# Moving the key-value products of one batch to another place among the next batch's matmuls

## The chip, the cores and the metric

The kernel runs on one core of a Trainium2 chip. The metric is the device time of one launch in microseconds, the median of several runs. TensorE (PE in the profile) does the matmuls, ScalarE (ACT), VectorE (DVE) and GpSimd (POOL) the rest, and SyncE (SP) issues the DMAs. Every engine works through its own fixed list of instructions and waits on semaphores for the others.

## What is computed

Eight batches of 256 rows by 512 columns go through linear cross attention with 16 heads, and then through a feed-forward layer with quantised activations and ternary weights. Cut to what matters here:

```
q, k, v = heads(layernorm(x) @ Wq.T + bq), heads(ctx @ Wk.T + bk), heads(ctx @ Wv.T + bv)
q_prime = relu(q @ Wqf.T)                 # 64 features per head
k_prime = relu(k @ Wkf.T) * mask
kv      = einsum('bhnf,bhne->bhfe', k_prime, v)       # "products of features and values"
k_sum   = k_prime.sum(rows)
x       = x + (q_prime @ kv / (q_prime @ k_sum + 1e-8)) @ Wo.T + bo
# feed-forward: weights and activations quantised, wq(w) has values -1, 0, 1 times mean|w|
h       = bit_linear(layernorm(x), w_up) * relu(bit_linear(layernorm(x), w_gate))**2
x       = x + bit_linear(rms(h) * subln_weight, w_down)
```

## The kernel before

The whole program is unrolled. Python first writes a list of steps (class `Plan`, lines 93 to 237); each has a lane (pe, act, dve, pool, sp), a cost, and the steps it waits for. The PE lane is executed in the order in which the steps were added. The order on the other lanes is worked out by `Plan.queues` (line 108): it simulates the engines with the costs of the table `COST` (line 55) and gives each engine, whenever it is free, the step that can start first, and among these the one that is needed first. The order is fixed when the kernel is built, so moving a step on the PE lane may also reorder the other lanes.

The work falls in two stages. First, for each batch b from 0 to 6, the loop at lines 840 to 855 adds to the PE lane:

- `keys(b)` (line 504): 48 matmuls of 128x256, each product in three parts (high*high, high*low, low*high). ACT then adds the bias and copies the result from PSUM to SBUF (`kT{b}.*.all`). Below K0, K1, ...
- `values(b, t)` for t = 0 and 1 (line 527): two halves of 12 matmuls of 128x512 each. DVE adds the bias and writes the rows (`v{b}.{t}.rows`). Below V0, V1, ... for the two halves together.
- `kv(b - 1)` (line 573): the products of the features and values of the batch before; 64 steps in fp32, of which each becomes two matmuls, 128 small ones of 33 columns. They wait for the four `kf{b-1}.{r}.rows` of DVE and for the rows of the values, write PSUM banks 0 and 1, and ACT copies them out (`kv{b-1}.0`, `kv{b-1}.1`). Below kv0, kv1, ...
- `features(b)` (line 549): 64 steps, again 128 small matmuls, of 64 columns, into banks 0 to 3; they wait for the keys' copies and for whoever used those banks last. DVE turns them into `kf{b}.{r}.rows` (line 567). Below F0, F1, ...

So in the kernel before, the PE order of a batch is keys, first half of the values, products of the batch before, second half of the values, features. `means(b, stage)` (line 481) stands between them. After three of these places it sets a weight of the feed-forward layer (gate, up, down) to ternary: DVE adds up four partial sums (`w{w}.sum`), a one-column matmul on PE (`w{w}.all`, line 470) adds them over partitions, DVE makes mean and scale, ACT multiplies four chunks of the weight (`w{w}.{c}.fma`), DVE rounds them (`w{w}.{c}.min`, `.tern`). The place (5, "kv") belongs to the down weight; each `.min` that finishes frees a 1 MB slot into which SP loads `x` or `Wo` for the next stage.

The last batch (7) and the second stage are written out by hand in `FLOW` (line 41), word by word: K is `keys`, V a range of the 24 value matmuls, F `features`, P `kv`, X transposes of normalised rows, L layer norm statistics, W queries, Q query features, A the attention products, S the output projection, G, U and D the feed-forward matmuls; `@` lists the PSUM banks to use.

Each PE matmul is two instructions, a weight load (LDWEIGHTS) and the matmul itself. At the start 13 matmuls warm PE up.

Of the kernel before, what the change touches and what calls it, by code (L numbers as in the profile page):

```python
# [38 lines left out]


FLOW = (
# [198 lines left out]
def xattn_bitffn_kernel(nc, x_d, ctx_d, wk_d, wv_d, wq_d, wo_d, feat_d, small_d, bv_d, bo_d, g_d, wg_d, wu_d, wd_d, out_d):  # L240
# [4 lines left out]
    with ExitStack() as es:  # L245
# [16 lines left out]
        AM, SXI, SX, SX3, CC, C2, S0, S1, SS, VE, RS, CRS, M0, M1, MX, SYI, SO, KK = range(18)  # L262
# [84 lines left out]
        def dma(name, mb, waits, out, in_, sem):  # L347
            if sem not in dma_names:
                dma_names.append(sem)
            return add("sp", name, 2.9 * mb, waits, lambda e: e.dma_start(out, in_), sem)  # L350

        def mm(name, cost, waits, out, lhsT, rhs, start, stop):
            return add("pe", name, cost, waits, lambda e: e.matmul(out, lhsT, rhs, start=start, stop=stop))  # L353
# [4 lines left out]
        def tt(lane, name, cost, waits, out, a, b, op):  # L358
            return add(lane, name, cost, waits, lambda e: e.tensor_tensor(out, a, b, op))  # L359

        def ts(lane, name, cost, waits, out, a, s1, s2, op0, op1):
            return add(lane, name, cost, waits, lambda e: e.tensor_scalar(out, a, s1, s2, op0, op1))  # L362
# [26 lines left out]
        def load_slot(name, s, src):  # L389
            return dma(name, 1.0, slot_user[s], slot[s], src, f"slot{s}")  # L390
# [22 lines left out]
        def ctx_load(b, n=1):  # L413
            w = KC * T // n
            for h in range(n):
                c = slice(w * h, w * h + w)
                dma(f"ctx{b}.in{h}", 0.5 / n, ctx_lo[b - 2] if b > 1 else [], craw[:, b % 2, c], ctx_d[b][:, c], f"ctx{b % 2}.{h}")

        def ctx_split(b, n=1):
            war = [f"v{b - 2}.1.3.2"] if b > 1 else []  # L420
            w = KC * T // n
            ctx_lo[b] = []
            for h in range(n):
                o = slice(w * h, w * h + w)
                c = slice(1024 * (b % 2) + w * h, 1024 * (b % 2) + w * h + w)
                act(f"ctx{b}.hi{h}", 0.06 + w * 8.7e-4, [f"ctx{b}.in{h}"] + war, aph[:, c], craw[:, b % 2, o], ACT.Copy)
                ctx_lo[b].append(tt("dve", f"ctx{b}.lo{h}", 0.07 + w * 1.04e-3, [f"ctx{b}.in{h}", f"ctx{b}.hi{h}"] + war, apl[:, c], craw[:, b % 2, o], f32(aph[:, c]), ALU.subtract))
# [30 lines left out]
        def ternary_load(w):  # L458
            for c in range(4):
                s = chunk_slot[c]  # L460
                ld = load_slot(f"w{w}.{c}", s, raw_d[w][:, c * 2048:c * 2048 + 2048])
                act(f"w{w}.{c}.abs", 1.85, [ld], tern[w][:, c * 2048:c * 2048 + 2048], slot[s], ACT.Abs, accum_out=wsum[:, 4 * w + c:4 * w + c + 1])

        def ternary(w, b):
            q = 4 * w
            add("dve", f"w{w}.sum", 0.07, [f"w{w}.{c}.abs" for c in range(4)],
                lambda e: e.tensor_reduce(wst[:, q:q + 1], wsum[:, q:q + 4], AX_X, ALU.add))

            total = ps[:, b, 511:512]
            mm(f"w{w}.all", 0.25, [f"w{w}.sum", "ones"] + bank_user[b], total, wst[:, q:q + 1].broadcast_to((P, P)), vt[:, 0, 0, 32:33], True, True)  # L470
            bank_user[b] = [ts("dve", f"w{w}.mean", 0.1, [f"w{w}.all"], wst[:, q + 2:q + 3], total, 1.0 / (FI * H), 1e-5, ALU.mult, ALU.max)]
            recip(f"w{w}.scale", 0.07, [f"w{w}.mean"], wst[:, q + 3:q + 4], wst[:, q + 2:q + 3])
            for c in range(4):
                s = chunk_slot[c]
                t = tern[w][:, c * 2048:c * 2048 + 2048]
                act(f"w{w}.{c}.fma", 1.95, [f"w{w}.scale", f"w{w}.{c}.abs", "cm0"], slot[s], slot[s], ACT.Identity, scale=wst[:, q + 3:q + 4], bias=cm[:, 0:1])
                ts("dve", f"w{w}.{c}.min", 1.13, [f"w{w}.{c}.fma"], t, slot[s], MAGIC, 1.0, ALU.subtract, ALU.min)
                slot_user[s] = [f"w{w}.{c}.min"]
                add("dve", f"w{w}.{c}.tern", 0.6, [f"w{w}.{c}.min"], lambda e, t=t: e.tensor_scalar(t, t, -1.0, None, ALU.max))

        def means(b, stage):

            if (b, stage) in TERNARY_AFTER:
                w = TERNARY_AFTER.index((b, stage))
                ternary(w, {"keys": 4, "kv": 2, "values": 6}[stage])
                if w < 2:
                    ternary_load(w + 1)
                else:
                    ts("pool", "CW", 0.3, ["w0.mean", "w1.mean"], CW, Mg, Mg, Mu, ALU.mult, ALU.mult)
                    load_slot("Wo", 3, wo_d)  # L490
                    for n in range(6):
                        dma(f"x{n}", 0.5, slot_user[n // 2], xs[:, 2 * n:2 * n + 2, :], x_d[n], f"x{n}")
                    ln1(0)
# [33 lines left out]
        def values(b, t):  # L527

            c0 = 1024 * (b % 2)
            out = ps[:, 4 + t, :]  # L530
            calls = []
            for kc in range(KC):
                cs = slice(c0 + T * kc + P * t, c0 + T * kc + P * t + P)
                for z in range(3):
                    def call(kc=kc, cs=cs, z=z):
                        waits = [Wv_lo[kc]] + ctx_lo[b] + (bank_user[4 + t] if kc == z == 0 else [])
                        left, right = apl if z == 2 else aph, wol if z == 1 else woh
                        last = kc == KC - 1 and z == 2
                        (open_banks.remove if last else open_banks.add)(4 + t)
                        k = mm(f"v{b}.{t}.{kc}.{z}", 0.23, waits, out, left[:, cs], right[:, kc, :], kc == z == 0, last)  # L540
                        if last:
                            dst = vt[:, (2 * b + t) % 4, :, :].rearrange("p a (c d) -> p a c d", c=2)[:, :, :, 0:32]
                            src = out.rearrange("p (a c d) -> p a c d", a=NP, c=2)
                            bvv = bv_b[:, :].rearrange("p (a c d) -> p a c d", a=NP, c=2)
                            bank_user[4 + t] = [tt("dve", f"v{b}.{t}.rows", 0.62, [k, "bv", "ones"], dst, src, bvv, ALU.add)]
                    calls.append(call)
            return calls
# [63 lines left out]
        def ln1(a):  # L611
            for t in range(2):
                i = 2 * a + t
                r = ln_stats(0, i, [f"x{a}"])
                war = [f"xT{i - 2}.3"] + ([f"oT0.{t}.hi", f"oT0.{t}.lo"] if a == 1 else []) if a else [f"warm{WARM - 1}"]
                ts("dve", f"xn{i}", 0.34, [r, f"ln0.{i}.agg"] + war, xn[:, t, :], xs[:, i, :], mv[:, 0, i, 0:1], rstd[:, 0, i:i + 1], ALU.subtract, ALU.mult)
# [213 lines left out]
        def run_all(calls):  # L830
            for call in calls:
                call()
# [7 lines left out]
        for b in range(last):  # L840
            keys(b)
            means(b, "keys")
            if b >= 1:
                ctx_load(b + 1)
            else:
                ctx_split(1)
            run_all(values(b, 0))
            if b:
                run_all(kv(b - 1))
            means(b, "kv")  # L850
            run_all(values(b, 1))
            means(b, "values")
            if b >= 1:
                ctx_split(b + 1)
            features(b)
# [96 lines left out]
```

How the kernel before makes its waits and increments, by code:

```python
        def run(lane, eng):  # L209
            seen = {}
            for i in order.get(lane, []):
                _, name, _, waits, fn, dma = self.steps[i]
                need = {}
                for w in waits:
                    s, v = at[w]
                    if need.get(s, (0, None))[0] < v:
                        need[s] = (v, w)
                for s, (v, _) in need.items():
                    if seen.get(s, 0) < v:
                        eng.wait_ge(s, v)
                        seen[s] = v
                last = fn(eng)
                if dma is not None:
                    last.then_inc(dma_sems[dma], 16)
                elif name in at:
                    last.then_inc(sems[lane], 1)
# [6 lines left out]
        def sync(e):  # L233
            run("sp", e)
            e.wait_ge(dma_sems["out"], issued["out"])
```

## Time and profile before

| | us |
|---|---|
| median of 3 runs | 433.4 |
| runs | 433.19, 435.17, 433.4 |
| the profiled execution | 431.52 |
| its span, first to last instruction | 429.4 |
| stage of keys, values and features, up to the end of F6 | about 113 |

The profile is one execution. Its page gives each engine's busy time; the timeline lists instructions in order of time with the idle time before each and what ended it. "issue" there means that the engine waited for nothing that the profile shows. The windows give each engine's busy time, the clock granted to TensorE (1.00 is 2.4 GHz) and the busy share of the 16 DMA engines in a stretch.

### The profile page before, as it was taken

The page shows a single profiled execution, that of the slowest core. Times are in us where ns is not written, and L with a number is a line of the kernel's source. Part 1 is how long each engine was busy: PE and PEld are TensorE (multiplying, and loading weights), DVE is VectorE, ACT ScalarE, POOL GpSimd, SP SyncE. Part 2 cuts the span into 40 slices and gives each one's busy share as a digit, 9 for nine tenths or more (in the row PEclk, how much of TensorE's full clock was granted, in tenths as well). Part 3 has the DMA queues.
Part 4 walks back from the last instruction along what each step waited for, and adds up shares of the span by engine and source line. Part 5 has one row for each costly group of instructions (what it writes and reads, how often), then busy time and mean ns, then how long its engine had stood idle before and what let it go on. Part 6 is the DMA issues. An engine that isn't in the chain of part 4 may idle for free.

```text
span 429.4 us, 11234 instructions
## 1 busy us (share of the span) xinstructions
PE 412.2 (96%) x4804; PEld 283.6 (66%) x4835; DVE 342.8 (80%) x505; ACT 286.6 (67%) x406; POOL 147.8 (34%) x290
## 2 busy tenths in 40 slices
PE   8998899899998999999999999999999999999995
PEld 5887799788878855844674576476467466464443
DVE  4634837629969959998997898899998898998983
ACT  5674968858145277779529656855973978949970
POOL 0000000002353542374282535637225533444660
PEclk9999989999999999999999999999999999999999
DMA  7992652804602110023213033031303120423055
GB/s 226 417 416 74 248 197 84 362 2 130 267 5 81 45 27 2 12 51 87 51 41 82 0 84 76 14 74 40 63 24 63 38 49 16 85 75 63 13 119 151
DMA packets 51170, 42.42 MB, mean 99 GB/s; under 512 B 43056, under 2 KB 44080, under 8 KB 49200
## 3 DMA queue, kind: packets, MB, share of 16 engines
q1 hardware_dynamic: 51120, 41.70, 32.0%
q8 instruction: 38, 0.62, 0.6%
q14 instruction: 12, 0.10, 0.1%
HBM read 27.01 MB, written 4.19 MB: 73 GB/s over the span
## 4 chain that ended last, share of the span: by engine, by line
PE 60%; DVE 16%; POOL 7%; ACT 7%; issue 6%; DMA 3%; SPq 0%; DVEq 0%; POOLq 0%; ACTq 0%
PE ps L353 50%; DVE zb L359 3%; PE ps L561 3%; DVE rows_of L365 3%; PE ps L683 2%; POOL tk L362 2%; ACT rb L356 2%; PE ps L588 2%; DMA xqT<-xqb 2%; PE ps L660 2%; DVE tk L767 2%; ACT kT L356 1%; POOL zb L359 1%; DVE rows_of L359 1%; PE ps L622 1%
## 5 line engine op out<-in xcount | busy, mean ns | idle before, releaser
L353 PE MATMUL ps<-tg,xqT 128*128 128x512 bf16 x243 | 58.1, 380 | 2.5 <-DMA xqT<-xqb 1.1
L353 PE MATMUL ps<-tu,xqT 128*128 128x512 bf16 x245 | 59.2, 380 | 1.2 <-issue 0.6
L362 POOL TENSOR_SCALAR tk<-tk 128x1 f32<-128x1 f32 x96 | 39.2, 409 | 35.8 <-DVE tk L718 18.1
L353 PE MATMUL ps<-td,yqT 128*128 128x512 bf16 x202 | 45.9, 380 | 0.5 <-issue 0.2
L353 PEld LDWEIGHTS ps<-tu,xqT 128*128 128x128 bf16 x256 | 24.2, 98 | 31.1 <-issue 2.1
L356 ACT ACTIVATE rb<-zb 128x1024 f32<-128x1024 f32 x29 | 30.6, 1055 | 20.8 <-DVE zb L359 20.6
L353 PEld LDWEIGHTS ps<-tg,xqT 128*128 128x128 bf16 x256 | 23.5, 98 | 31.1 <-issue 2.4
L359 DVE TENSOR_TENSOR zb<-ps,rb 128x1024 f32<-128x1024 f32 x29 | 35.3, 1217 | 6.6 <-ACT rb L356 6.5
L353 PE MATMUL ps<-aph,wqh 128*128 128x256 f32 x128 | 37.3, 291 | 0.0
L767 DVE TENSOR_REDUCE tk<-zb 128x1 f32<-128x1024 f32 x30 | 36.2, 1208 | 1.0 <-POOL zb L359 0.8
L353 PE MATMUL ps<-aph,wkh 128*128 128x256 f32 x128 | 36.7, 291 | 0.1
L353 PE MATMUL ps<-apl,wkh 128*128 128x256 f32 x128 | 35.9, 284 | 0.5 <-issue 0.5
L359 POOL TENSOR_TENSOR zb<-zb,g_b 128x1024 f32<-128x1024 f32 x9 | 21.7, 2408 | 42.0 <-ACT rb L356 18.5
L353 PE MATMUL ps<-aph,wql 128*128 128x256 f32 x128 | 36.0, 281 | 0.0
L353 PE MATMUL ps<-apl,wqh 128*128 128x256 f32 x128 | 36.0, 281 | 0.0
L353 PE MATMUL ps<-aph,wkl 128*128 128x256 f32 x128 | 35.8, 283 | 0.0
L353 PEld LDWEIGHTS ps<-td,yqT 128*128 128x128 bf16 x208 | 19.9, 98 | 24.0 <-issue 0.7
L362 POOL TENSOR_SCALAR lnv<-mv 128x1 f32<-128x1 f32 x32 | 9.7, 304 | 71.0 <-DVE mv L607 68.8
L356 ACT ACTIVATE rb<-ps 128x1024 f32<-128x1024 f32 x29 | 29.5, 1018 | 5.5 <-PE ps L353 4.6
L356 ACT ACTIVATE rb<-rb 128x1024 f32<-128x1024 f32 x29 | 30.7, 1059 | 0.6
L359 DVE TENSOR_TENSOR zb<-zb,g_b 128x1024 f32<-128x1024 f32 x21 | 26.0, 1243 | 2.5 <-ACT rb L356 2.5
L353 PE MATMUL ps<-woh,qoh 128*128 128x512 f32 x64 | 27.0, 423 | 0.7 <-DVE qol L365 0.5
(134 smaller groups left out, 1039.5 us busy)
## 6 DMA issues: line engine op xcount, KB each, us to landing
xs<-in_wg_dram SPq DMA_DIRECT2D x4, 1024.0 KB, 14.1
xs<-in_wu_dram SPq DMA_DIRECT2D x4, 1024.0 KB, 6.4
xs<-in_wd_dram SPq DMA_DIRECT2D x4, 1024.0 KB, 6.8
xs<-in_x_dram SPq DMA_DIRECT2D x8, 512.0 KB, 4.9
out_dram<-xs SPq DMA_DIRECT2D x15, 256.0 KB, 2.2
craw<-in_ctx_dram SPq DMA_DIRECT2D x7, 512.0 KB, 6.9
xs<-in_wk_dram SPq DMA_DIRECT2D x4, 256.0 KB, 4.4
xs<-in_wv_dram SPq DMA_DIRECT2D x4, 256.0 KB, 5.8
```

The costliest lines, as they stand in the source:

```text
L353: return add("pe", name, cost, waits, lambda e: e.matmul(out, lhsT, rhs, start=start, stop=stop))
L356: return add("act", name, cost, waits, lambda e: e.activation(out, in_, func, **kw))
L359: return add(lane, name, cost, waits, lambda e: e.tensor_tensor(out, a, b, op))
L362: return add(lane, name, cost, waits, lambda e: e.tensor_scalar(out, a, s1, s2, op0, op1))
L365: return add("dve", name, cost, waits, lambda e: e.scalar_tensor_tensor(out, a, s, b, op0, op1))
L561: add("pe", f"kf{i}.{q}.{r}.{c}", 0.015, waits, lambda e, out=out, left=left, right=right, at=(32 * r, 64 * c): e.matmul(out, left, right, ...
L588: k = add("pe", f"kv{b}.{pr}.{t}.{c}", 0.018, waits, lambda e: e.matmul(out, left, right, start=t == 0, stop=t == 1, tile_position=(0, 32 ...
L622: add("pe", f"{tag}.{kc}", 0.11, (waits + bank_user[b] + ["small"]) if kc == 0 else [], lambda e, out=out, src=src: e.transpose(out, src, ...
L660: add("pe", f"qf{a}.{q2}.{r}.{c}", 0.0535, waits, lambda e, out=out, left=left, right=right, at=(32 * r, 64 * c): e.matmul(out, left, righ ...
L683: add("pe", f"at{a}.{n}.{q2}.{r}.{hd}", 0.055, waits, lambda e, out=out, left=left, right=right, at=(64 * hd, 32 * r): e.matmul(out, left, ...
L767: add("dve", f"ym{u}", 1.15, [f"Y{u}"], lambda e: e.tensor_reduce(col(M0 + h, i), zs, AX_X, ALU.max, apply_absolute_value=True))
```

## The change

The products of features and values of batch b - 1 stand directly behind the keys of batch b, and both halves of the values of batch b follow. The step `means(b, "kv")` goes with the products. In the last batch the products of batch 6 (P6) move from between K7 and F7 to a place before the last quarter of the values, `V12.18`.

```diff
 FLOW = (
-    "X0@6 V0.4 X1@7 V4.8 V8.12 L1 V12.18 W0.0@6 W0.1@7 Q0@0123 V18.24 A0@0123 K7 P6 F7 X2@5 S0@4 P7 ...
+    "X0@6 V0.4 X1@7 V4.8 V8.12 L1 P6 V12.18 W0.0@6 W0.1@7 Q0@0123 V18.24 A0@0123 K7 F7 X2@5 S0@4 P7 ...
@@
             else:
                 ctx_split(1)
-            run_all(values(b, 0))
             if b:
                 run_all(kv(b - 1))
             means(b, "kv")
+            run_all(values(b, 0))
             run_all(values(b, 1))
             means(b, "values")
```

## Rows read from the trace of the kernel before

**Rows 1.** The page's first part: busy us (share), number of instructions.

```profile
PE 412.2 (96%) x4804; PEld 283.6 (66%) x4835; DVE 342.8 (80%) x505; ACT 286.6 (67%) x406; POOL 147.8 (34%) x290
```

**Rows 2.** Waits of PE, whole span: total us, times, longest.

```profile
PE ps L561 <- issue: 5.3, 4, 1.6
...
PE ps L353 <- DVE wst L362: 0.2, 1, 0.2
```

**Rows 3.** The page's DMA queues, the one for instructions: packets, MB, share.

```profile
q8 instruction: 38, 0.62, 0.6%
```

**Rows 4.** PE's timeline, F0 to F2: start, us, what, [idle before <- releaser].

```profile
17.54 1.60 PE L561 MATMUL ps<-fkr,kT 32*64 32x64 f32 x128
...
20.96 0.38 PE L353 MATMUL ps<-apl,wkh 128*128 128x256 f32 x1 [0.46 <-issue]
...
28.38 1.40 PE L588 MATMUL ps<-vt,kp 128*32 128x33 f32 x128
...
32.66 0.93 PE L561 MATMUL ps<-fkr,kT 32*64 32x64 f32 x66
34.90 0.90 PE L561 MATMUL ps<-fkr,kT 32*64 32x64 f32 x62 [1.31 <-issue]
...
44.76 1.40 PE L588 MATMUL ps<-vt,kp 128*32 128x33 f32 x128
...
49.01 1.51 PE L561 MATMUL ps<-fkr,kT 32*64 32x64 f32 x119
52.10 0.35 PE L561 MATMUL ps<-fkr,kT 32*64 32x64 f32 x9 [1.58 <-issue]
```

**Rows 5.** PE's timeline, kv3 to F5, without the large matmuls.

```profile
76.68 1.40 PE L588 MATMUL ps<-vt,kp 128*32 128x33 f32 x128
...
80.96 1.29 PE L561 MATMUL ps<-fkr,kT 32*64 32x64 f32 x101
83.79 0.47 PE L561 MATMUL ps<-fkr,kT 32*64 32x64 f32 x27 [1.54 <-issue]
...
97.10 1.59 PE L561 MATMUL ps<-fkr,kT 32*64 32x64 f32 x128
```

**Rows 6.** PE's timeline, kv6 (P6) and F7.

```profile
134.94 1.40 PE L588 MATMUL ps<-vt,kp 128*32 128x33 f32 x128
136.76 1.61 PE L561 MATMUL ps<-fkr,kT_last 32*64 32x64 f32 x114 [0.41 <-ACT kvc L356]
139.20 0.37 PE L561 MATMUL ps<-fkr,kT_last 32*64 32x64 f32 x14 [0.83 <-issue]
```

**Rows 7.** Windows: busy us (instructions) of PE, PEld, DVE, ACT, POOL; clock, DMA, GB/s.

```profile
26.00:33.00 7.00, 7.00 (x184) 5.50 (x183) 2.12 (x3) 5.19 (x9) 0.00 (x0) 1.00 0.95 387
...
46.50:52.00 5.50, 4.02 (x131) 3.20 (x130) 5.35 (x7) 5.50 (x5) 0.00 (x0) 1.00 0.99 366
52.00:56.00 4.00, 3.90 (x27) 3.83 (x27) 4.00 (x7) 1.43 (x2) 0.00 (x0) 0.58 1.00 365
...
74.00:84.00 10.00, 8.46 (x276) 6.75 (x279) 6.01 (x8) 8.68 (x12) 0.00 (x0) 1.00 0.98 401
...
99.00:103.00 4.00, 4.00 (x38) 4.00 (x37) 3.97 (x7) 4.00 (x5) 0.00 (x0) 1.00 0.82 262
...
117.50:137.00 19.50, 19.09 (x341) 16.04 (x342) 14.99 (x29) 11.07 (x22) 8.93 (x18) 1.00 0.05 18
```

**Rows 8.** DVE's timeline: the down weight's mean, its first rounded chunk.

```profile
94.34 0.16 DVE L362 TENSOR_SCALAR wst<-ps 128x1 f32<-128x1 f32 x1 [0.95 <-PE ps L353]
...
96.86 1.23 DVE L362 TENSOR_SCALAR td<-xs 128x2048 bf16<-128x2048 f32 x1 [2.17 <-ACT xs L356]
```

**Rows 9.** The queue of SP: the first two loads of x.

```profile
98.12 1.59 SPq L350 DMA_DIRECT2D xs<-in_x_dram  x2
```

**Rows 10.** ACT's timeline: the copies of the second half of K7.

```profile
135.72 0.82 ACT L356 ACTIVATE kT_last<-ps,small 128x256 f32<-128x256 f32 x2
```

**Rows 11.** DVE's timeline: the four rows of the features of batch 7.

```profile
139.51 2.48 DVE L365 SCALAR_TENSOR_TENSOR kp<-ps,small 128x512 f32<-128x512 f32 x4
```

2 rows, old and new, of the table FLOW are left out of this document.

## The prediction

> **What bounds the kernel now.** I read the page's busy times first: PE is busy for 412.2 of 429.4 us [rows 1]. In the first stage every other engine has gaps, so a microsecond that PE loses there is lost at the end too, unless the second stage has slack of its own. So the question is which idle time of PE the change removes and which it makes. The waits of PE answer the first half [rows 2]: the longest by far is 5.3 us in four pieces ahead of the features' matmuls (L561), put down to "issue", so no semaphore ended them. Beside these stand 0.41 us ahead of F7 for the copies of P6 [rows 6] and 0.25 us for the mean of the first weight [rows 2].
>
> The timeline shows where they lie: 1.31 us after 66 matmuls of F1, 1.58 after 119 of F2, 1.54 after 101 of F4, 0.83 after 114 of F7, and a small one of 0.46 after 10 matmuls of K1 [rows 4 to 6]. Counting matmuls from the start (13 of warming up, 48 + 24 + 128 in batch 0, 48 + 24 + 256 in each later one, 2 for each weight's sum) these are numbers 223, 479, 862, 1502 and 2653. Their distances are 256, 383, 640 and 1151, that is 2, 3, 5 and 9 times 128, less at most one. A matmul and its weight load are two instructions, so PE stops only at multiples of 256 instructions. The instruction queue carries 0.62 MB in 38 packets [rows 3], 16 KB each, for some 9,640 instructions of PE [rows 1]: 64 bytes apiece, 255 to a packet. I take it that PE runs out of instructions: a block is consumed before the next one is there.
>
> How long a block takes can be bounded from rows. Let a boundary be entered when the matmul behind it starts, and look how long after that the next one opened, where PE had to wait. The boundary before F1's lies 90 matmuls into kv0, at 29.4; it opened at 34.90: 5.5 us. Before F4's: kv3 after 125 matmuls, at 78.1, to 83.79: 5.7. Before F7's: kv6 after 107, at 136.1, to 139.20: 3.1. The first two ran with the DMA engines 95 to 98% busy, the last one mostly with idle ones (5%) [rows 4 to 7]. K1's needed only 3.3 us (10 matmuls into F0, at 17.7, to 20.96), though large loads ran then as well. So I use 3.1 us with free queues and 5.6 under loads, and the second is not always reached.
>
> **The change part by part.** Work is the same, matmul by matmul; only the order changes. From the rows: kv 1.40, features 1.59, half of the values (80.96 - 76.68 - 1.40) 2.88, and keys 97.10 - 84.26 - 2 x 2.88 - 1.40 - 0.1 = 5.6 [rows 5]. Every boundary stays at the same matmul number. Features stay at the same numbers too, but now 24 long matmuls stand between kv and features in place of 12.
>
> F1: from kv0's boundary to F1's take 0.4 + 5.7 + 0.8 = 6.9 us, over 5.6: the 1.31 go. But kv0's boundary, now right behind K1, comes 38 x 0.117 + 1.0 = 5.4 us after the late one of K1 (20.96), against up to 5.7 to 6 in these loads: a new wait of 0 to 0.6, I take 0.5. Gain 0.8.
>
> The first weight's mean: `w0.all` stays behind K2, but V2, which must wait for that bank, now has kv1 (1.40) ahead of it. The 0.25 and the restart are hidden: 0.3.
>
> F2: the boundary before it stays 9 long matmuls away, at V2's sixteenth, and 2.2 + 1.5 = 3.7 us would be too short again. But PE's sequencer reads ahead while long matmuls run: kv1's third matmul (44.8) and V2's sixteenth (44.76 + 1.40 + 3 x 0.24 = 46.9) are successive boundaries 2.1 us apart, and PE did not stop there [rows 4]. In the kernel before only three long matmuls stand ahead of this boundary, and small ones before those; after it fifteen do, so it is entered some 3 us earlier, ahead of the loads that fill the queues from 46.5 on [rows 7]. Bounds 0 and 1.58; I take the whole 1.58. With it goes what followed: the window from 52 to 56 has a granted clock of 0.58, that is mostly 1.2 GHz, after small matmuls and the wait. It did 18 key matmuls in 3.55 us that cost 18 x 0.116 = 2.1 at 2.4 GHz: 1.5.
>
> F4: now 6.9 us from kv3's boundary: 1.54 go.
>
> P6 and F7: the wait of 0.41 and F7's of 0.83 go, because blocks are read ahead during K7. But P6 covered something. The second half of K7 is copied out at 135.72 to 136.54, and F7 needs that after 32 of its matmuls [rows 10]; without P6 between, F7 waits some 0.7 for it. And at0 with its chain on DVE and ACT comes 1.4 later against F6, so the four rows of F7 (2.48 us, done at 141.99 [rows 11], before P7) come up to 1.1 later against PE. I book 0 for the end of batch 7 (-0.6 to +0.6).
>
> The four rows of the other features (2.48) must now fit behind 5.6 us of keys instead of 8.5. They start with the features' end, so 3.1 us are left for other DVE work; if that cover is gone, kv waits for what is missing. I book 0. P6 has at least 3 us of values and the transposes over the rows of F6: 0, at worst 0.6.
>
> The down weight: its mean comes 2.88 earlier against F5, and so the first rounded chunk (96.86 to 98.09) and the loads of x behind it (from 98.12) [rows 8, 9]. SP is not held by anything else. These loads filled the queues at 99 to 103 (0.82 [rows 7]), under K6; now they start before F5. Boundaries lie 27 matmuls into F5, 27 into K6 and 107 into kv5. F5 to K6 takes 1.3 + 3.1 = 4.4 us against 5.6 (-0.1 if short loads hold nothing up, 2.2 at the longest): a wait of 1.4. K6 to kv5, formerly with half of the values between, takes 2.4 + 1.2 = 3.6: nothing if the queues are free by then (3.1), 2.0 to 2.4 if the loads of Wo and the next x follow at once. The row for that is the same 99 to 103, busy but not full; I take 1.2, the middle.
>
> Sum: 0.8 + 0.3 + 1.6 + 1.5 + 1.5 = 5.7 gained, 1.4 + 1.2 = 2.6 given back: 3.1. The profiled execution would fall from 431.5 to 428.4 (span 426.3). It was shorter than each of the runs (433.19 to 435.17), so I subtract from the median: 430.3.
>
> The Trainium skill's page "Runtime: NRT & Kernel Launch", section "Instruction fetch mechanics", says that instructions come in 16 KiB blocks of 256, and that fetching them is hidden because the sequencer issues more slowly than blocks arrive. The first half agrees with the packets of this trace (0.62 MB in 38), the second does not fit waits at multiples of 128 matmuls. By that rule the change would save no such wait; that is the second rival.
>
> **The rivals.** First, both new waits at their full length (2.2 + 2.4) and batch 7 dearer by 0.6: 5.7 - 5.2 = 0.5 gained, 432.9. For it: loads of 4 MB follow each other there. Opposite to it, neither new wait comes: 427.7.
>
> Second, the waits belong to the features themselves and move with them, and fetching is hidden: then only the 0.3 for the mean is won, 433.1. Against it speaks the count.
>
> Third, slower: fetches wait behind loads wherever these run. The place is V2 to F2 and F5 to kv5; it decides whether a block is asked for before or after the first load of the group starts. If after, F2 keeps its 3.1 (wait and slow clock), F5 to kv5 pays 4.6, and PE, idle among small matmuls, falls to 1.2 GHz once more for 1.5: 5.7 - 3.1 - 4.6 - 1.5 = -3.5, so 436.9. For it speaks that F2's boundary was entered just about when the loads began.
>
> **How the numbers follow.** The forecast gets 0.38, no new wait 0.19, full new waits 0.2, waits that move with the features 0.08, slower 0.15. A measurement of this kernel can tell about 0.5%, 2.2 us: faster is below 431.2, slower above 435.6. The forecast and no new wait lie below it nearly always (0.56 in all); full new waits, the second rival and a part of the slower one within (0.31); the rest above (0.13). The range goes from 427.2, with nearly no new wait, to 434.8, through the full waits and the mild half of the slower case.
>
> **What would show it.** Right: "issue" ahead of F1, F2, F4 and F7 gone, the clock 1.00 in K3, a short one in kv0; waits, if any, 27 matmuls into K6 and 107 into kv5. Wrong: "issue" still in F2, waits of kv on DVE's rows, a wait of the down weight's sum, or a gain in the first stage that is lost after it.

## The result, and the profile after

The changed kernel takes 429.57 us, the median of 18 runs (427.89 to 432.73); the kernel before, in 18 runs with it, 432.96 (429.93 to 435.56). The ratio is 0.9942 with a 95% interval of 0.9919 to 0.9965: 0.6% faster, some 2.5 us. The profiled execution has a span of 428.0 us against 429.4.

First the waits of PE, whole span (total us, times, longest), as in [rows 2]:

```profile
PE ps L588 <- issue: 3.4, 3, 1.8
...
PE ps L353 <- issue: 1.2, 2, 0.8
...
PE ps L561 <- ACT kT_last L356: 0.6, 1, 0.6
```

The 5.3 us ahead of the features (L561) are gone, and so are the 0.25 for the first weight's mean and the 0.41 for P6's copies. In their place stand 3.4 us in the products (L588) and 1.2 in key matmuls (L353). Of the last, 0.79 lie in K1, where the kernel before had waited too (0.46 [rows 4]). PE's timeline shows where; these lines answer to [rows 4 to 6]:

```profile
21.94 0.39 PE L353 MATMUL ps<-apl,wkh 128*128 128x256 f32 x1 [0.79 <-issue]
...
28.14 0.55 PE L588 MATMUL ps<-vt,kp 128*32 128x33 f32 x38 [0.69 <-issue]
...
48.78 1.59 PE L561 MATMUL ps<-fkr,kT 32*64 32x64 f32 x128
...
77.91 1.59 PE L561 MATMUL ps<-fkr,kT 32*64 32x64 f32 x128
...
92.30 1.59 PE L561 MATMUL ps<-fkr,kT 32*64 32x64 f32 x128
...
97.67 0.39 PE L353 MATMUL ps<-aph,wkh 128*128 128x256 f32 x1 [0.40 <-issue]
...
100.26 1.22 PE L588 MATMUL ps<-vt,kp 128*32 128x33 f32 x107
103.31 0.39 PE L588 MATMUL ps<-vt,kp 128*32 128x33 f32 x21 [1.84 <-issue]
...
134.43 0.72 PE L561 MATMUL ps<-fkr,kT_last 32*64 32x64 f32 x32
135.72 1.48 PE L561 MATMUL ps<-fkr,kT_last 32*64 32x64 f32 x96 [0.58 <-ACT kT_last L356]
...
140.47 1.15 PE L588 MATMUL ps<-vt,kp 128*32 128x33 f32 x98
142.48 0.45 PE L588 MATMUL ps<-vt,kp 128*32 128x33 f32 x30 [0.85 <-issue]
```

F2, F4 and F5 run through in one piece of 1.59 us. The waits that remain stand 10 matmuls into K1, 90 into kv0, 27 into K6, 107 into kv5 and 98 into P7. By the count of the prediction these are the matmuls 223, 351, 1886, 2014 and 2781: again multiples of 128 apart, less at most two. Nothing outside this grid says "issue" for more than 0.2 us.

The trace also has the blocks themselves: every packet of the instruction queue ([rows 3], 16 KB each) has a start and a length there. Each of these five waits ends 1.3 to 1.6 us after such a packet has landed, and each of the five in the kernel before 1.2 to 1.5. The packet for kv5, for instance, starts at 100.84, 3.2 us after PE entered the block before it (97.67) and just as the loads end; it takes 0.9 us, and PE goes on at 103.31.

How the stretch goes can be read from the starts: F5 from 97.10 to 92.30, F7 from 136.76 to 134.43. So 4.8 us were won by batch 5 (and 0.6 more, because this execution began its first features 0.64 later, at 18.18), and half of it was given back in batch 6. The windows of the same execution:

```profile
50.00:56.00 6.00, 6.00 (x85) 5.81 (x80) 6.00 (x9) 5.92 (x7) 0.00 (x0) 1.00 0.99 369
91.50:100.00 8.50, 8.10 (x179) 7.40 (x178) 8.47 (x14) 5.57 (x5) 0.77 (x2) 1.00 0.99 349
100.00:109.00 9.00, 7.16 (x155) 5.94 (x154) 5.46 (x14) 1.33 (x4) 3.60 (x8) 1.00 0.07 25
137.00:140.00 3.00, 3.00 (x30) 2.52 (x22) 3.00 (x7) 0.60 (x1) 1.68 (x1) 1.00 0.93 326
```

K3 has the full clock now (1.00, where [rows 7] show 0.58). The loads of x and Wo fill the queues from 91.5 to 100 (0.99), that is under F5 and K6, where the blocks for K6 and kv5 have to be fetched; in the kernel before they ran in three groups from 99 on.

### The profile page after: what moved, and what is told of

It reads as the page before. It is cut to its first block, busy times and chain, and to the rows that moved or that the text cites. A ratio compares the mean times of both kernels' runs of the same rounds, so it can differ in the third digit from the quotient of the medians.

```text
span 428.0 us, 11266 instructions
## 1 busy us (share of the span) xinstructions
PE 414.2 (97%) x4835; PEld 282.6 (66%) x4835; DVE 341.2 (80%) x505; ACT 287.0 (67%) x406; POOL 145.4 (34%) x290
## 4 chain that ended last, share of the span: by engine, by line
PE 58%; DVE 17%; ACT 8%; POOL 6%; issue 5%; DMA 5%; SPq 0%; DVEq 0%; POOLq 0%; ACTq 0%
PE ps L353 48%; DVE zb L359 3%; DVE rows_of L365 3%; PE ps L561 2%; PE ps L683 2%; POOL tk L362 2%; PE ps L588 2%; ACT rb L356 2%; DMA xs<-in_wu_dram 2%; PE ps L660 2%; DVE tk L767 2%; ACT kT L356 2%; POOL zb L359 1%; DMA xqT<-xqb 1%; PE ps L622 1%
## 5 line engine op out<-in xcount | busy, mean ns | idle before, releaser
L353 PE MATMUL ps<-tg,xqT 128*128 128x512 bf16 x256 | 60.6, 380 | 0.8 <-DMA xqT<-xqb 0.7
L353 PE MATMUL ps<-tu,xqT 128*128 128x512 bf16 x256 | 60.6, 379 | 0.2 <-DVE zb L359 0.2
L353 PE MATMUL ps<-td,yqT 128*128 128x512 bf16 x208 | 46.9, 379 | 0.0
L353 PEld LDWEIGHTS ps<-tu,xqT 128*128 128x128 bf16 x256 | 24.3, 98 | 31.1 <-issue 2.1
L353 PEld LDWEIGHTS ps<-tg,xqT 128*128 128x128 bf16 x256 | 23.5, 98 | 30.8 <-issue 2.5
L353 PE MATMUL ps<-aph,wkh 128*128 128x256 f32 x128 | 36.2, 287 | 1.5 <-DVE wkl L359 0.6
L353 PE MATMUL ps<-aph,wqh 128*128 128x256 f32 x128 | 37.1, 290 | 0.0
L353 PE MATMUL ps<-apl,wkh 128*128 128x256 f32 x128 | 35.2, 279 | 0.8 <-issue 0.8
L353 PEld LDWEIGHTS ps<-td,yqT 128*128 128x128 bf16 x208 | 19.8, 98 | 24.3 <-issue 0.7
L353 PE MATMUL ps<-apl,wqh 128*128 128x256 f32 x128 | 35.8, 280 | 0.0
L353 PE MATMUL ps<-aph,wql 128*128 128x256 f32 x128 | 35.8, 280 | 0.0
L353 PE MATMUL ps<-aph,wkl 128*128 128x256 f32 x128 | 35.1, 278 | 0.0
L359 DVE TENSOR_TENSOR vt<-ps,bo_b 128x512 f32<-128x512 f32 x16 | 11.0, 688 | 22.5 <-PE ps L353 22.4
L359 POOL TENSOR_TENSOR xs<-xs,bo_b 128x512 f32<-128x512 f32 x16 | 21.7, 1359 | 20.7 <-DVE xn L362 12.6
```

## The experiments

My theory: PE stands still where a block of 256 instructions is consumed before the next has come; a block comes later when large loads are on the queues; and the change helps by putting more time between two such boundaries. Rivals: the waits belong to the small matmuls themselves, P6 brings the gain, or the place of the boundaries decides alone. Times are medians beside runs of the kernel before on the same chip, and each ratio is to those runs; versions of the changed kernel were not all timed beside each other.

**The two parts of the change, each alone.** The loop's part (P6 as before); the edit is against the changed kernel, cut:

```diff
-    ... L1 P6 V12.18 ... A0@0123 K7 F7 ...
+    ... L1 V12.18 ... A0@0123 K7 P6 F7 ...
```

> The loop's part of the change alone; P6 stays between K7 and F7. My theory: the whole gain is in the loop (waits of F1, F2, F4 for instructions and the slow clock in K3 gone, shorter new ones in kv0, K6 and kv5) and the end of batch 7 is worth nothing: 2 to 3.5 us faster than before, within 0.6 us of the whole change; F7 waits 0.4 us for the copies of P6 again and some 0.8 us for instructions after 114 matmuls. Rival (P6 brings a part of the gain): at least 1 us slower than the whole change.

It took 429.15 us, ratio 0.9927 (0.9897 to 0.9958) to before. Features 1 to 6 had no wait; F7's two came back (0.33 and 1.19), kv5 waited 2.38, and K6, for which I had written a wait, had none. The move of P6 alone, with the loop of before:

> The move of P6 alone; the loop stays as before. My theory: the waits of F1 (1.3 us), F2 (1.6) and F4 (1.5) stay, F7's two waits (0.41 and 0.83) go, one of about 0.6 for the keys' copies and one in P7 come: within 0.6 us of before. Rival (P6 pays): 1 us or more faster than before.

It took 433.18 us, ratio 1.0015 (0.9988 to 1.0041). F2 and F4 kept their waits (1.88 and 1.45), F1 only 0.23, and P7 waited 0.85. And a wait came that I had not expected, in P6 itself (PE's timeline):

```profile
115.69 0.75 PE L588 MATMUL ps<-vt,kp 128*32 128x33 f32 x62
118.40 0.78 PE L588 MATMUL ps<-vt,kp 128*32 128x33 f32 x66 [1.97 <-issue]
```

62 matmuls in, matmul 2269, on the grid. The windows show the loads still running ahead of it (0.67; the packet of this block starts at 116.14, as they end) and TensorE at 0.58 of its clock behind it:

```profile
111.00:118.00 7.00, 5.43 (x175) 4.42 (x162) 7.00 (x15) 1.20 (x2) 0.08 (x1) 1.00 0.67 256
119.00:123.00 4.00, 4.00 (x34) 3.46 (x22) 3.83 (x11) 0.28 (x1) 3.25 (x10) 0.58 0.01 4
```

So the whole gain is in the loop. In the whole change P6 costs nothing, because there the loads of x are over before it (at 113, P6 starts at 114.63); without the loop's part they are not.

**Loads held back.** The changed kernel, but x0 waits for kv5, Wo and x1 to x5 for P6, x6 and x7 for P7 (lines cut at the dots).

```diff
-load_slot("Wo", 3, wo_d)
-for n in range(6):
-    dma(f"x{n}", 0.5, slot_user[n // 2], ...)
+dma("x0", 0.5, slot_user[0] + ["kv5.7.1.3"], ...)
+slot_user[3] = slot_user[3] + ["kv6.7.1.3"]
+load_slot("Wo", 3, wo_d)
+for n in range(1, 6):
+    dma(f"x{n}", 0.5, slot_user[n // 2] + ["kv6.7.1.3"], ...)
...
-    dma(f"x{b}", 0.5, slot_user[b // 2], ...)
+    dma(f"x{b}", 0.5, slot_user[b // 2] + [f"kv{NB - 1}.7.1.3"], ...)
```

> The changed kernel with six loads held back: x0 until kv5 is done, Wo and x1 to x5 until P6 is done, x6 and x7 until P7 is done; nothing else. My theory (a block of instructions comes late because it waits behind these loads): the waits 27 matmuls into K6 (0.40), 107 into kv5 (1.84) and 98 into P7 (0.85) all vanish, and the kernel is 2 to 3 us faster than the whole change, some 5 us faster than before. Rival (3.6 us is too short for 128 small matmuls whatever the queues do, or small matmuls stop PE for another reason): the waits stay, above all the 1.84 in kv5, and the time is that of the whole change or longer, since the loads come later.

428.49 us, ratio 0.9915 (0.9883 to 0.9946). All three waits vanished, as the theory said: from 88 to 104 us PE was busy without a break, with the DMA engines 12% busy. The packets for K6 and kv5 now start 0.8 and 0.1 us after the block before is entered, where they started 2.7 and 3.2 us after it. But only some 1 us of the expected 2 to 3 arrived. The late loads pushed the layer norms of the next stage into the attention of batch 0, and F7 now waited for DVE; behind that the clock was 0.66 over 5 us. Of the 12 runs 7 have a mean clock of 0.996. The other five have a median of 427.5 us, 2 us below the changed kernel's runs at the full clock (429.5). PE's timeline, and two windows:

```profile
132.75 0.33 PE L563 MATMUL ps<-fkr,kT_last 32*64 32x64 f32 x4 [1.20 <-DVE xn L359]
133.34 0.45 PE L563 MATMUL ps<-fkr,kT_last 32*64 32x64 f32 x20 [0.27 <-DVE xn L359]
134.37 1.48 PE L563 MATMUL ps<-fkr,kT_last 32*64 32x64 f32 x96 [0.58 <-ACT kT_last L356]
```

```profile
88.00:104.00 16.00, 16.00 (x338) 14.17 (x337) 12.46 (x16) 9.76 (x11) 0.00 (x0) 1.00 0.12 36
...
136.00:141.00 5.00, 5.00 (x49) 3.83 (x48) 3.30 (x7) 0.60 (x1) 2.71 (x2) 0.66 0.01 3
```

**kv5 alone back between the halves.** The changed kernel, but in batch 6 half of the values stands again ahead of the products.

```diff
+if b == NB - 2:
+    run_all(values(b, 0))
 if b:
     run_all(kv(b - 1))
 means(b, "kv")
-run_all(values(b, 0))
+if b < NB - 2:
+    run_all(values(b, 0))
```

> The changed kernel, but kv5 alone stands again between the two halves of V6. The loads stay where they are. My theory (what counts is the time from one boundary of 256 instructions to the next): 2.9 us more lie between K6's boundary and kv5's, so the 1.84 in kv5 go and the 0.40 in K6 stay; 1 to 2 us faster than the whole change. Rival (the wait belongs to kv5's small matmuls while loads run): about 1.8 us stay in kv5.

427.46 us, ratio 0.9882 (0.9841 to 0.9923): 2.1 us below the changed kernel's 429.57, in six runs at another time; the intervals of the two ratios just overlap (0.9942 has 0.9919 to 0.9965). kv5 ran through; K6 kept a wait of 0.29 and P7 one of 1.11:

```profile
96.10 0.39 PE L353 MATMUL ps<-aph,wkh 128*128 128x256 f32 x1 [0.29 <-issue]
...
101.51 1.40 PE L588 MATMUL ps<-vt,kp 128*32 128x33 f32 x128
...
139.41 0.45 PE L588 MATMUL ps<-vt,kp 128*32 128x33 f32 x30 [1.11 <-issue]
```

The loads and the small matmuls are the same as in the changed kernel; only the distance of the boundaries in K6 and kv5 grew.

**The same with x6 and x7 held back until P7.** The edit is the last one of the loads held back.

> kv5 between the halves of V6, as in the run before, and the loads of x6 and x7 wait until P7 is done. My theory: the wait in P7 (1.1 us in that run) goes, but the time stays within 0.4 us of that run's 427.5, because the first gate matmuls wait for the transposed rows anyway (0.78 us in that run) and just wait longer. Rival (the wait in P7 is worth its length): about 1 us faster.

P7 ran through, and the time was 426.7 us, ratio 0.9897 (0.9865 to 0.9929), 0.76 below the run before it on other runs of the kernel before, whose own ratio is a little better (0.9882). By the profile the rival is right: the first gate matmuls still waited for the transposed rows (0.64 in place of 0.78), yet the stretch from the start of the first output projection to them took 13.95 us in place of 15.42. P7's wait held up the transposes behind it, DVE's list takes their result before the steps on the way to the gate (it waited 0.76 us for them in the run before, and not here), and so it did lie on the path. The two times are too close, in 6 runs each, to say how much it is worth.

**And with P6 where it was before**, between K7 and F7:

> The loop as changed but kv5 between the halves of V6, and P6 between K7 and F7 as before. My theory (where P6 stands is worth nothing): 427 to 428.5 us, within 0.6 of the run with P6 moved; waits of some 0.35 us ahead of F7 and 1 us in it. Rival (the moved P6 brings a part): 429 us or more.

427.47 us, ratio 0.9903 (0.9876 to 0.993), waits of 0.32 ahead of F7 and 0.99 in it: with the loop in this shape the place of P6 is worth nothing that can be measured, as in the theory.

**One load moved in the kernel before.** g, which the first stage does not use, waits for half of V3.

```diff
-dma("g", 1.0, [], g_b[:, :], g_d, "g")
+dma("g", 1.0, ["v3.0.3.2"], g_b[:, :], g_d, "g")
```

> The kernel before with one load moved: g (1 MB, used only in the second stage) waits until the first half of V3 is done, so it is taken from the loads of the first 33 us and runs at about 63 to 66 us, when the queues were idle. My theory (loads hold up the block of instructions): F1's wait of 1.31 shrinks to under 0.6, and F3, which did not wait, waits about 1 us (0.6 to 1.5) 45 matmuls in, since its boundary comes only 4.4 us after that in kv2; F2's and F4's waits stay. Rival (the loads have nothing to do with it): F1 keeps 1.3 us and F3 stays without a wait.

One run, 430.33 us. F1 had no wait at all, and F3, which did not wait in the profile of the kernel before, waited 1.26 us after 45 matmuls. PE's timeline, then the window in which g was loaded:

```profile
33.55 1.59 PE L561 MATMUL ps<-fkr,kT 32*64 32x64 f32 x128
...
63.79 0.75 PE L561 MATMUL ps<-fkr,kT 32*64 32x64 f32 x45
65.80 1.14 PE L561 MATMUL ps<-fkr,kT 32*64 32x64 f32 x83 [1.26 <-issue]
```

```profile
60.20:63.50 3.30, 3.30 (x69) 2.79 (x57) 0.16 (x1) 1.51 (x4) 0.00 (x0) 1.00 0.84 318
```

A load of 1 MB made a wait of 1.26 us where none had been. That it also took the one from F1 is less plain by the wait alone, since F1 waited only 0.23 with P6 moved and g in its old place: PE came to kv0's block 1 us later there, as it did here (0.9). The packets decide it: F1's starts at 32.60 in the kernel before and at 32.43 with P6 moved, as the first loads end, and at 30.87 with g held back; F3's starts 3.5 us after the block before is entered in place of 0.8. F4 kept 1.44; F2 had 0.59, less than I had written.

**Boundaries moved.** The changed kernel with 16 tiny matmuls ahead of the warming up, so that every boundary comes 16 matmuls earlier in the work.

```diff
+for n in range(16):
+    mm(f"tiny{n}", 0.03, ["zeros"], ps[:, 7, 0:32], zeros[:, 0:128], zeros[:, 128:160], True, True)
 for n in range(WARM):
```

> The changed kernel with 16 tiny matmuls (32 columns) ahead of the warming up; they take about 0.5 us before the first data land. Every boundary of 256 instructions moves 16 matmuls to the front of the work. My theory: the waits move with them: 82 matmuls into P7 (not 98) some 0.8 us, and the boundary that lay 27 matmuls into K6 now lies 11 into K6, only 2.7 us after the one before it and under the loads of x, so a wait of 1 to 3 us there, and 0 to 1 us 91 matmuls into kv5 (5.3 us after K6's). Rival (the waits belong to certain matmuls or to a semaphore that the profile does not show): they stay 27 matmuls into K6, 107 into kv5 and 98 into P7, with 0.4, 1.8 and 0.8 us.

One run, 425.84 us. The waits did not stay at their matmuls, so that rival is out; but the 1 to 3 us that I expected in K6 did not come either, nor those in kv5 and P7. Of "issue" only 0.2 us was left, in F0 (waits of PE, longest first):

```profile
PE ps L353 <- DMA yqTq<-yqb: 1.6, 1, 1.6
...
PE ps L561 <- ACT kT_last L356: 0.6, 1, 0.6
...
PE ps L561 <- issue: 0.2, 1, 0.2
```

What I had left out of this expectation is the reading ahead that I had used for F2: the boundary 11 matmuls into F5 stands close behind V5's long matmuls, so PE's sequencer is at it before the loads of x begin, while 27 matmuls in it is not. The packet for K6 agrees: here it starts at 88.66, 1.9 us before PE enters that block of F5 (90.61), in the changed kernel at 95.21, 2.7 us after it (92.54). Timed:

> The changed kernel with the 16 tiny matmuls ahead of the warming up once more, now timed. In its one look no wait for instructions of more than 0.3 us was left. My theory: the waits in kv0, K6, kv5 and P7 (together 2 to 4 us in the changed kernel) stay away and no slow clock follows them, so 425 to 427 us, 3 to 4 us faster than the changed kernel, without any change in the order of the work. Rival (that look was a lucky one): 428.5 us or more.

427.14 us, ratio 0.9899 (0.9875 to 0.9922). This execution had waits of 1.18 in F0, 0.50 in kv1 and 0.62 in P7, all on the moved grid; K6 and kv5 ran through. So the single run was a lucky one in part, but a gain stands, 2 to 2.5 us below the changed kernel and not 3 to 4. The kernel before with the same 16:

> The kernel before with the same 16 tiny matmuls. My theory: the order of before puts features 12 long matmuls behind the products, so F1, F2 and F4 find their boundary 4.2 to 4.3 us after the one before it (kv0 after 62 matmuls to F1 after 50, kv1 after 115 to F2 after 103, kv3 after 97 to F4 after 85) and wait about 1 to 1.6 us each, as without the shift: within 1 us of before. Rival (where the boundaries lie decides alone, and the order of the work does nothing): 3 us or more faster than before, like the changed kernel with the shift.

430.69 us, ratio 0.9988 (0.9967 to 1.0008). The waits moved by 16 and stayed:

```profile
35.40 1.10 PE L561 MATMUL ps<-fkr,kT 32*64 32x64 f32 x78 [1.26 <-issue]
...
51.54 0.46 PE L561 MATMUL ps<-fkr,kT 32*64 32x64 f32 x25 [0.49 <-issue]
...
81.43 0.73 PE L561 MATMUL ps<-fkr,kT 32*64 32x64 f32 x43 [1.22 <-issue]
```

They stand after 50, 103 and 85 matmuls, each 16 earlier than in [rows 4, 5]; F2's is 0.49, less than the 1 us that I had written. F0 and F7 wait 1.03 and 1.05, also on the moved grid. With the order of before this move of the grid does nothing that can be measured. With 48 tiny matmuls the changed kernel did this:

> The changed kernel with 48 tiny matmuls in place of 16. My theory, with the sequencer some 22 matmuls ahead: the boundaries in front of long matmuls are entered early enough, those in V5, F5 and kv5 lie 6.3 us or more apart, and only two are short under loads: F6 after 35 to P6 after 14 (5.0 us, a wait of 0.3 to 0.8) and F7 after 66 to P7 after 50 (4.6 us, 0.5 to 1.3); 425.5 to 428 us. Rival (positions do not predict the waits): waits elsewhere, or about the 429.6 us of the changed kernel.

427.2 us, ratio 0.9897 (0.9871 to 0.9924). The time was inside what I had given, the places were not: P6 and P7 ran through, and F3 waited 1.24 after 125 matmuls, with idle queues (0.00 from 62 to 64.5). That block was asked for just as the loads of the second weight ended; that the block before it was itself late and so stopped the reading ahead would fit (its packet landed at 59.21, F3's starts at 61.97), but no run tests it.

## Why the prediction held, and where it did not

I gave 430.3 with 427.2 to 434.8, faster; it is 429.57. That it is so near is in part luck. Between the two profiled executions the span fell by 1.4 us, not by the 3.1 of the sum: P7's 0.85, 0.33 more in K1 and a start 0.64 later were not in it. The medians differ by 3.4, since the profiled execution of the kernel before was faster than its median (431.52) and that of the changed kernel slower (430.05). By its steps:

- **What bounds the kernel.** Right, and shown: every wait on "issue" above 0.2 us of the changed kernel, of each part and of the shifted kernels lies on the grid of 256 instructions, the grid moves with tiny matmuls, and one 1 MB load held back made a wait of 1.3 us in F3. In all traces of these kernels each wait on the grid ends 1.2 to 1.6 us after a packet of the instruction queue has landed. Under loads it is the start of the packet that comes late, up to 4.9 us after PE enters the block before (P6 moved alone) against 0.9 with idle queues (F7 in the kernel before); the packet itself takes about 1 us either way. The lengths that I had worked out were a little short: I had counted two boundaries by the changed order. In the kernel before they lie 78 matmuls into kv0 and 113 into kv3, which gives 5.7 and 5.9 us in place of 5.5 and 5.7.
- **F1, F2, F4, the mean.** Right: all gone (1.31, 1.58, 1.54, 0.25). F2 lies only 3.4 us behind its boundary and still does not wait in the changed kernel, nor in the loop's part alone, the loads held back and kv5 between the halves. The reason given, that the sequencer reads ahead among long matmuls, shows in the packets: F2's starts at 46.03, 0.6 us before PE enters the block ahead of it (46.65) and before the loads; in the kernel before it starts at 49.71, 2.8 us after (46.88).
- **kv0 and K1.** 0.5 was booked for kv0, 0.69 measured. Nothing was booked for K1, ahead of which the change moves nothing; it waits 0.46 before, 0.79 after, 0.91 with P6 moved and not at all with x6 and x7 held back. Differences of a few tenths in one profile therefore say little.
- **The slow clock in K3.** 1.5 booked; K3 has the full clock. But I took a drop for certain that the runs show only often: each run lists its mean granted clock, and of the 29 runs of the kernel before beside the first four experiments 24 had 0.996 or less, of the 18 of the changed kernel 5. Four thousandths less are one drop as in [rows 7] (0.42 of the clock over 4 of 430 us): medians of before 430.3 us at 1.00, 432.1 at 0.996, 434.7 at 0.992. The changed kernel has 431.4 (0.996 and less) and 429.5 (1.00). From these figures I estimate that some 1.5 us of the difference between the two kernels are fewer drops. At the full clock the change brings only about 0.8, in runs at different times; the loop's part alone, on the same chip as those 29, brings 1.6 (428.7).
- **K6 and kv5.** 1.4 and 1.2 booked, 0.40 and 1.84 measured (2.38 in the loop's part alone). Both places right and the sum nearly so (2.24 for 2.6), but by luck, since the two terms were mis-sized in opposite directions. K6's 1.4 did not even follow from my own lengths (5.6 less 4.4 is 1.2), and in the loop's part alone K6 had no wait. K6's block came less late than the 5.6 us under loads, 5.1 after its boundary, and kv5's, 5.6 after, came at the long end.
- **Batch 7.** P6 and F7 behaved as booked: 0.83 and 0.41 gone, 0.58 for the keys' copies. What failed is that I gave the fetch for P7 no price: the block after F7's comes 4.6 us behind it, under the loads of x6 and x7 (0.93), and P7 waits 0.85.
- **The rivals.** Waits near their full length (432.9) came in kv5 alone; no new wait there (427.7) is nearly what kv5 between the halves shows, 427.46. That the waits belong to the features themselves is refuted. The Trainium skill's page "Runtime: NRT & Kernel Launch", section "Instruction fetch mechanics", says that instructions come in blocks of 256 and that fetching them is hidden. The blocks are right, but here PE waited up to 2.4 us for one.
- **The slower case** did not come, since the block for F2 is asked for ahead of the loads; but a piece of it appeared when P6 moved alone: 1.97 us of waiting in P6 and a clock of 0.58 behind it.

All the versions of the changed kernel with kv5 between the halves or with moved boundaries, 426.7 to 427.5 us, lie below both kernels. Against the changed kernel this rests on runs at different times (ratios 0.9882 to 0.9903 against 0.9942, some of whose intervals overlap).

## What to carry to other kernels

When PE waits on "issue", count matmuls between such waits: equal distances speak of instruction blocks, and then what helps is time between two boundaries, long matmuls just ahead of a boundary, and no large loads while a block is fetched. Where the trace lists the packets of the instruction queue, see whether each wait ends shortly after one has landed. Groups of a hundred small matmuls should stand apart, with long ones between. A step that is moved forward takes the loads behind it forward too, here under the next block's fetch.

## What the runs showed of the hardware that I had not expected

- The same kernel waits differently from run to run at the same boundaries (16 tiny matmuls: 0.2 us in one execution, 2.3 in another).
- A wait among small matmuls can cost twice: of the executions shown, the kernel before (1.58 in F2), P6 alone (1.97), the loop's part alone (2.38 in kv5) and the loads held back (1.20 for DVE) had a clock of 0.58 to 0.71 behind it over 4 to 5 us, which is mostly 1.2 GHz; other waits of that size, as 1.84 in kv5 of the changed kernel or 1.88 in F2 with P6 moved, were not followed by that.
- Bringing waits to nothing does not bring their length: 3.1 us of waits removed by holding loads back were worth some 1 us, or 2 among runs at the full clock.
